# Wider handshakes in the first pass, separate rings for the one-hots of the counts, and 14 places in the last pass of a four-layer graph kernel

## The reference

```python
h = relu(layernorm(x)); x = x + relu(segment_sum((h @ W0)[src] * edge_weight, dst))
h = relu(layernorm(x)); x = x + relu(segment_sum(norm * (h @ W1.T + b1)[src], dst))   # norm = deg^-1/2 of both ends
h = relu(layernorm(x)); x = x + relu((h + segment_sum(h[src], dst)) @ G1 + g1) @ G2 + g2
h = relu(layernorm(x)); x = x + attention(h)   # 8 heads: softmax over the edges of a target, weighted sum of rows
```

## Time and profile before

| | us |
|---|---|
| median of 3 runs | 2899.95 |
| the profiled execution | 2903.65 |
| its span | 2902.3 |
| PE busy in the span | 2502.0 (86%) |
| DVE busy | 1822.8 (63%) |
| POOL busy | 873.2 (30%) |
| first pass, window 124:814 | 690 |
| counts, window 814:1140 | 326 |
| last pass, window 2317:2897 | 580 |

### The profile page before, as it was taken

The page is one execution under the profiler, slowest core; times in us unless marked ns, Lnnn a source line. Parts: engine busy times, 40 slices in busy tenths (PEclk is TensorE's granted clock), DMA queues, the critical chain, the costliest instruction groups (busy, mean ns, idle before and its releaser), DMA issues.

```text
span 2902.3 us, 38667 instructions
## 1 busy us (share of the span) xinstructions
PE 2502.0 (86%) x9907; PEld 1393.7 (48%) x9907; DVE 1822.8 (63%) x4596; ACT 614.9 (21%) x1144; POOL 873.2 (30%) x900
## 2 busy tenths in 40 slices
PE   6888888878878888999989999998888799888787
PEld 5534444433333233666656555665688533333332
DVE  7765569668567775657343333344777687776666
ACT  4554420000036563000000000000555200000000
POOL 0366665666600000000000000000101366666665
PEclk9899988989987778999999999998999899999989
DMA  6586664555625444344711122111655367776665
GB/s 160 163 249 178 181 181 138 165 167 165 178 48 108 63 63 74 86 119 114 195 47 54 54 59 60 55 40 33 171 153 151 104 197 206 206 232 192 192 191 170
DMA packets 157069, 389.13 MB, mean 134 GB/s; under 512 B 44859, under 2 KB 46260, under 8 KB 156881
## 3 DMA queue, kind: packets, MB, share of 16 engines
q0 software_dynamic: 72400, 232.34, 28.1%
q1 hardware_dynamic: 83798, 153.04, 21.1%
q10 hardware_dynamic: 683, 1.28, 0.2%
HBM read 333.81 MB, written 52.72 MB: 133 GB/s over the span
## 4 chain that ended last, share of the span: by engine, by line
PE 55%; DVE 20%; issue 10%; DMA 7%; another core or an unknown queue 4%; POOL 2%; ACT 1%; SPq 0%; DVEq 0%; ACTq 0%
PE banks L2013 16%; PE banks L1876 15%; PE banks L2007 7%; PE banks L1842 7%; PE banks L2190 4%; DMA ring<-edge_counts 3%; DMA ring<-table,src_t 2%; DVE sel L1134 2%; POOL ring L2346 2%; DVE spare L1061 1%; PE banks L1831 1%; DVE spare L1059 1%; DVE rstd L898 1%; DVE stage L868 1%
## 5 line engine op out<-in xcount | busy, mean ns | idle before, releaser
L1876 PE MATMUL banks<-ring,sel 128*125 128x512 f32 x1682 | 895.1, 660 | 150.8 <-issue 96.1
L1876 PEld LDWEIGHTS banks<-ring,sel 128*125 128x125 f32 x1682 | 289.1, 200 | 467.4 <-issue 464.1
L2292 POOL DMA_INDIRECT ring<-table,src_t x440 | 435.1, 989 | 253.1 <-PE banks L1876 107.8
L2324 POOL DMA_INDIRECT x<-table,src_t x25 | 24.1, 962 | 1441.9 <-ACT spare L1775 1436.1
L2346 POOL DMA_INDIRECT ring<-table,src_t x401 | 386.6, 964 | 217.1 <-issue 97.2
L2013 PE MATMUL banks<-acc,ring 125*125 125x512 f16 x1900 | 438.5, 381 | 8.1 <-DVE ring L1262 6.6
L2013 PEld LDWEIGHTS banks<-acc,ring 125*125 125x125 f16 x1900 | 257.2, 137 | 161.9 <-issue 29.0
L1613 DVE TENSOR_TENSOR ring<-ring,banks 128x512 f32<-128x512 f32 x388 | 255.0, 683 | 118.2 <-DMA ring<-table,src_t 100.7
L2007 PE MATMUL banks<-spare 128*125 128x450 f16 x590 | 262.6, 511 | 52.3 <-DVE spare L1061 25.2
L2007 PEld LDWEIGHTS banks<-spare 128*125 128x125 f16 x590 | 93.0, 158 | 222.4 <-issue 220.7
L1842 PE MATMUL banks<-wh,hTh 128*125 128x512 f32 x300 | 137.2, 457 | 68.3 <-DVE hTl L914 28.5
(11 more groups left out here) (411 smaller groups left out, 3117.2 us busy)
## 6 DMA issues: line engine op xcount, KB each, us to landing
ring<-edge_counts SPq DMA_DIRECT2D x35, 683.6 KB
edge_counts<-big SPq DMA_DIRECT2D x175, 97.7 KB
ring<-table,src_t POOLq DMA_INDIRECT x841
sel<-edge_counts SPq DMA_DIRECT2D x11, 683.6 KB
acc<-dst_places SPq DMA_DIRECT2D x28, 256.0 KB
x<-dst_places SPq DMA_DIRECT2D x27, 256.0 KB
acc<-src_digits SPq DMA_DIRECT2D x28, 224.0 KB
x<-src_digits SPq DMA_DIRECT2D x27, 224.0 KB
```

The source lines that it names most:

```text
L1876: last = P.matmul(to, sel[:, n % SELS, :], rows, start=False, stop=True, skip_group_check=True)
L2292: G.indirect_dma_start(out=ring[:, i % RING, :], out_offset=None, in_=table[0][:, :], in_offset=bass.IndirectOffsetOnAxis(ap=src_t[:, i:i ...
```

## The change

Four edits:

1. In the first pass PE's `project` moves from +13 to +16 and DVE's `next_made` from +22 to +25. The degree one-hots get four places instead of two, and DVE writes a group's at its step +2 instead of +4; it waits for the group four before it. Two of the places lie over arrays that are read until `deg_hot` is complete, so the third group waits for that too.
2. In the counts the one ring of 10 becomes a ring of 8 for the key one-hots and one of 20 for the low ones. The low batch stands before the wait for a key's place.
3. In the last pass the ring has 14 places: the 11 of `ring` and the first three rows of `spare`. Only the other three rows of `spare` are gathered early (steps 203, 211 and 219), so the ring has 404 rows to gather.
4. Three more semaphores tell of landings in the new places.

```diff
@@ -42,7 +42,7 @@
-    HOTS = 10
+    KEYS, LOWS = 8, 20
@@ -263,12 +263,12 @@
         LB = 5
-        key_hot = [flat_spare[:, n * KEY_W // 2:(n + 1) * KEY_W // 2].bitcast(F16) for n in range(HOTS)]
-        low_room = flat_spare[:, HOTS * KEY_W // 2:HOTS * KEY_W // 2 + HOTS * TN // 2].bitcast(F16).rearrange("p (n i) -> p n i", i=TN)
-        low_hot = [low_room[:, n, :] for n in range(HOTS)]
+        LOWS_AT = KEYS * KEY_W // 2
+        key_hot = [flat_spare[:, n * KEY_W // 2:(n + 1) * KEY_W // 2].bitcast(F16) for n in range(KEYS)]
+        low_room = flat_spare[:, LOWS_AT:LOWS_AT + LOWS * TN // 2].bitcast(F16).rearrange("p (n i) -> p n i", i=TN)
+        low_hot = [low_room[:, n, :] for n in range(LOWS)]
@@ -328,7 +328,8 @@
-        lo_hot = stage[:, 3 * STEPS:3 * STEPS + 2 * SB * 64].bitcast(BF16).rearrange("p (q n) -> p q n", n=128)
+        lo_hot = [flat_stage[:, at:at + SB * 64].bitcast(BF16).rearrange("p (e n) -> p e n", n=128)
+                  for at in (3 * STEPS, 3 * STEPS + SB * 64, 0, 2 * STEPS)]
@@ -525,23 +526,33 @@
-        IN_SPARE = range(3 + 8 * TILES, 3 + 8 * (TILES + 6), 8)
+        IN_SPARE = range(3 + 8 * TILES, 3 + 8 * (TILES + 3), 8)
...
-        early.update({i: spare[:, j, :] for j, i in enumerate(IN_SPARE)})
+        early.update({i: spare[:, 3 + j, :] for j, i in enumerate(IN_SPARE)})
...
+        last_rows = [ring[:, (STEPS + m) % RING, :] for m in range(RING)] + [spare[:, m, :] for m in range(3)]
+        LAST_RING = len(last_rows)
+
         def ring_use(i):
-            return LAST * STEPS + ring_steps.index(i)
+            return ring_steps.index(i)
+
+        def ring_got(m):
+            at = m % LAST_RING
+            slot = (STEPS + at) % RING if at < RING else at
+            used = len(range(slot, STEPS, RING)) if at < RING else 0
+            return got[slot], 16 * (used + m // LAST_RING + 1)
 
         def rows_at(i):
-            return early[i] if i in early else ring[:, ring_use(i) % RING, :]
+            return early[i] if i in early else last_rows[ring_use(i) % LAST_RING]
@@ -863,9 +874,11 @@
-                if g >= 2:
-                    V.wait_ge(deg_sum, g - 1)
-                V.tensor_tensor(lo_hot[:, i % (2 * SB):i % (2 * SB) + SB, 0:TN], iota_p[:, None, :].to_broadcast([CE, SB, TN]),
+                if g >= len(lo_hot):
+                    V.wait_ge(deg_sum, g - len(lo_hot) + 1)
+                if g == 2:
+                    V.wait_ge(deg_hot, TILES)
+                V.tensor_tensor(lo_hot[g % len(lo_hot)][:, :, 0:TN], iota_p[:, None, :].to_broadcast([CE, SB, TN]),
@@ -1051,14 +1064,14 @@
             def step_hots(j):
-                if j >= HOTS:
-                    V.wait_ge(built, j - HOTS + 1)
                 if j % LB == 0:
-                    if j >= HOTS:
-                        V.wait_ge(built, j - HOTS + LB)
-                    V.tensor_tensor(low_room[:, j % HOTS:j % HOTS + LB, :], low_names[:, None, :].to_broadcast([128, LB, TN]),
+                    if j >= LOWS:
+                        V.wait_ge(built, j - LOWS + LB)
+                    V.tensor_tensor(low_room[:, j % LOWS:j % LOWS + LB, :], low_names[:, None, :].to_broadcast([128, LB, TN]),
                                     low_t[:, j:j + LB, None].to_broadcast([128, LB, TN]), ALU.is_equal).then_inc(low_ok, 1)
-                V.tensor_scalar(out=key_hot[j % HOTS], in0=key_names, scalar1=key_t[:, j:j + 1], scalar2=None, op0=ALU.is_equal).then_inc(hot_ok, 1)
+                if j >= KEYS:
+                    V.wait_ge(built, j - KEYS + 1)
+                V.tensor_scalar(out=key_hot[j % KEYS], in0=key_names, scalar1=key_t[:, j:j + 1], scalar2=None, op0=ALU.is_equal).then_inc(hot_ok, 1)
@@ -1140,7 +1153,7 @@
-                if groups < SGROUPS and DEG_STEPS[groups] + 4 == i:
+                if groups < SGROUPS and DEG_STEPS[groups] + 2 == i:
@@ -1159,7 +1172,7 @@
-                k = ended.get(i - 22)
+                k = ended.get(i - 25)
                 if k is not None:
                     next_made(k)
@@ -1606,7 +1619,7 @@
-                    V.wait_ge(got[ring_use(i) % RING], got_value(ring_use(i)))
+                    V.wait_ge(*ring_got(ring_use(i)))
@@ -1960,7 +1973,7 @@
-                    degree_group(groups, groups % 2)
+                    degree_group(groups)
@@ -1969,7 +1982,7 @@
-                k = ended.get(i - 13)
+                k = ended.get(i - 16)
                 if k is not None:
@@ -2334,18 +2347,17 @@
-                if k >= RING:
-                    G.wait_ge(stepped, step_value(LAST * STEPS + ring_steps[k - RING]))
+                if k >= LAST_RING:
+                    G.wait_ge(stepped, step_value(LAST * STEPS + ring_steps[k - LAST_RING]))
```

18 lines of the change are left out of this document (8 added, 10 removed).

## The result

Side by side on one chip the changed kernel takes 2887.85 us and the kernel before 2904.01, medians of 12 runs each. The ratio is 0.9948, with a 95% interval of 0.9938 to 0.9959: 15 us less by the ratio, where 38 were forecast. The profiled execution took 2886.89 us, its span is 2885.6.

| us | before | after | difference | forecast |
|---|---|---|---|---|
| first pass | 688.4 | 669.2 | -19.2 | -24 |
| counts | 318.2 | 319.0 | +0.8 | -3 |
| last pass | 578.4 | 581.7 | +3.3 | -11 |

What follows compares the result with a forecast made beforehand. PE leads each stage but idles, waiting on late DVE handshakes and, in the last pass, scaled rows. 24 + 3 + 11 = 38 us less than 2903.65 gives 2865.65, median 2862 us; range 2842 to 2882, 8 in 10 2822 to 2895.

Steps and rivals of the forecast that it cites:

- Projection at +16: First pass: projecting three steps later removes 22 us of PE's 31.2 us idle ahead of projections; sign: under 12 left.
- Degree one-hots: First pass: four places, written two steps earlier, remove 14 of 30.2 us idle ahead of degree matmuls; DVE's hold largely goes.
- The price of `next_made`: First pass: DVE's later next_made delays the chain to PE's transposes, costing 12 us; idle there rises from 5 to about 15.
- The fourth rival: First pass: DVE's normalizing chain becomes the bound, reaching next_rows 5.6 us later; kernel 11 us slower, 2911 us; chance 0.07.
- the 24 us forecast for the first pass: First pass: sum of projection, degree one-hots and the cost of next_made, 22 + 14 - 12 us less.
- Counts: Counts: separate rings let DVE keep a lead of 8 keys; 3 us less, bounds 10 less and 5 more.
- Last pass: Last pass: three more ring places let POOL gather further ahead while PE stands; 11 us less, bounds 0 and 34.
- I take a third of 31.8: Last pass: a third of PE's 31.8 us of waits for DVE's scaling is saved, 11 us.
- The first rival: Last pass: the added places are worth nothing, POOL's issue time bounds the loop; sum 27, time 2873 us; chance 0.15.
- The page's rule: Last pass: a gather takes an estimated 2.6 us, so 11 places (nearly 14 us of issuing) cover landings; no gain.
- The second rival: Saved waits return at gathers or `sel` one-hots: first pass gives 5, counts 3, last pass nothing; 2892 us; chance 0.15.

Runs made afterwards that it cites:

- e16: Kernel before with DVE writing and PE multiplying only 64 of 450 columns of each key one-hot in the counts; ratio 0.9991, counts 315.6 us (chip D).
- e13: Kernel before with the last pass's 401 ring gathers as plain transfers of 128 consecutive rows; ratio 0.9498, last pass 438.3 us (chip D).
- e14: Kernel before with POOL waiting for the landing of every fifth ring gather in the last pass; ratio 1.0508, stage 727.7 us (chip D).
- the wider chain: First-pass edits plus transposes at +12, split +19, projection +17, next_made +26, against the kernel before; ratio 0.9968 (chip B), 0.9956 (chip D).

## Why the prediction was wrong

**Projection at +16** (22 of 31.2 us): the idle fell by 18.8, to 12.4, where under 12 was named. Alone, on chip A, it takes the idle to nothing (0.5 us) and gives the whole gain (0.9937, 18 us), though with its price it was to give 10.

**Degree one-hots** (14 of 30.2): the idle fell by 26, to 3.9, and DVE's hold from 42.3 to 4.4, more than forecast. Yet the edit alone gives nothing (1.0000 on chip B), and on top of the distance 3 us on chip A (678.4 to 675.4). The term took idle ahead of one group for time of the stage.

**The price of `next_made`** (12 us, idle ahead of the transposes to 15): it rose to 33.7, and 8 us ahead of the key transposes were not foreseen. The mechanism was the one forecast, a chain that ends too late, but the cover of the earlier trace rows was counted for a delay of 2.8 us only. In 12 of the 24 tiles PE now stands until the chain ends. On chip A 5 us of this come with the distance and 25 with the degree one-hots, which the forecast had as relieving DVE. The fourth rival, the chain as the bound, had this mechanism with too high a price.

So the 24 us forecast for the first pass and the 19.2 measured are near each other in part by luck: the distance with its price gave 18 us for 10, the degree places 0 to 3 us for 14. Only 9.6 us came as idle time, and as much in PE's busy time, for which there was no term (the mean of a projection matmul went from 498 to 474 ns); its cause is open.

**Counts** (3 less): nothing came. DVE's late one-hots fell by 10 us (25.2 to 15.2), and the stage did not follow, since PE's register instructions set its pace (e16).

**Last pass** (11 less): this is the step that failed, and 14 of the 23 us missing. "I take a third of 31.8" came true as a wait (34.2 to 20.5 us) and not at all as time. PE's 55 us without a name, which stood beside those 32, had no place in the term. 21 of them were waits for scaled rows as well, and fell to 16. But 26 of them were PE's slow phases, and rose to 38. In every kernel with 14 places they are longer than with 11 on the same chip: 153 us in sum against 127 in the first comparison, 213 against 123 to 130 on A, 167 and 224 against 141 and 158 on C. The runs show that gathering feeds the phases (e13, e14) and that the stage does not move. That the places lengthen them by letting POOL gather on is what the sums suggest; no run isolates it.

The first rival named the outcome of the last pass, that the loop is POOL's own. On chip B that is the bound by the numbers. On the others POOL has the same pace of 1.25 us a gather and stands for PE's phases besides. The page's rule, "DMA: Bandwidth & Descriptors" of the Trainium skill, "Anatomy of one DMA — SWDGE (gpsimd) path", gave the right answer, a ring worth nothing, by a reason that the runs do not bear out: a gather in a row of five landed 3.2 us after it, not 2.6, and though 8 places (10 us of issuing) would cover that too, the stage was longer with them. The same section counts the making of descriptors as small. In this case GpSimd is occupied for 0.96 us by a gather and for 0.54 by a plain transfer of the same bytes, and on chip B the gathers' pace is the bound.

The second rival, waits that come back elsewhere, was right for part of the first pass: PE's idle of 122 us stayed the same with the wider chain.

Of the kernels that compute the same sums none was shown to be faster than the changed one. The first-pass edits alone equal it.

## What to carry to other kernels

When waits named for an engine go and idle time without a name grows by as much, look in the timeline at what ended just before each unnamed wait did. If it is always the same instruction of another engine, as DVE's L918 here, the handshake has only moved. If it is none, look at how long the register instructions of the waiting engine's sequencer take before adding places. A distance is worth what the stage gives back when it is changed alone, not the idle ahead of one group. Time a change on more than one chip where a stage's unnamed idle is large.

## What the hardware showed that I had not expected

- PE's sequencer has phases in which a register instruction takes 0.70 us instead of 0.04. They occur in the first comparison and on chips A, C and D, in the two passes where POOL gathers (beyond these at most four such instructions in a kernel, all within 1.5 us of a gather), and go when each gather is a plain transfer (0 phases) or POOL pauses after every fifth (1 instruction), but not when a gather brings an eighth of the bytes (140 instructions).
- Chip B has none, though POOL gathers there for 475 us without a pause, and runs the kernel before in 2731 us, 6% less than the others' 2901 to 2924. Why is open, and 14 places were not run there.
- A wait of PE that the view names `<-issue` can be a plain wait for DVE: all 25.3 us ahead of the changed kernel's transposes are, and 21 of the 55 us in the last pass of the kernel before.
- With plain transfers the last pass takes 438 us instead of 581, at a granted clock of 1.00. That bounds what fewer or cheaper gather instructions could give; none was tried.
